# Weighed sums of a windowed attention as three products of split operands

## The reference

```python
q = (x @ Wq.T).reshape(B, T, H, Dh).transpose(0, 2, 1, 3)     # 16 heads of 128
k = (x @ Wk.T).reshape(B, T, Hkv, Dh).transpose(0, 2, 1, 3)   # 4 key heads
v = (x @ Wv.T).reshape(B, T, Hkv, Dh).transpose(0, 2, 1, 3)
q = _rms_norm(q, qn_w); k = _rms_norm(k, kn_w)                # then both are rotated
scores = jnp.einsum('bhgtd,bhkd->bhgtk', qg, k)
mask = (dist >= 0) & (dist <= WINDOW)                         # WINDOW = 64
att = jax.nn.softmax(jnp.where(mask, scores, min), axis=-1)
ctx = jnp.einsum('bhgtk,bhkd->bhgtd', att, v)
return out @ Wo.T                                             # out: ctx, heads side by side
```

## Time and profile before

| | |
|---|---|
| median of 3 runs | 1400.53 us (1397.14 to 1403.43) |
| the profiled execution | 1384.34 us |
| its span, first to last instruction | 1382.5 us |
| mean granted clock of PE | 0.949 |
| busy, share of the span | PE 88%, PEld 68%, DVE 69%, ACT 55%, POOL 44% |

### The profile page before, as it was taken

The page is one execution under the profiler, slowest core; times in us unless marked ns, Lnnn a source line. Parts: engine busy times, 40 slices in busy tenths (PEclk is TensorE's granted clock), DMA queues, the critical chain, the costliest instruction groups (busy, mean ns, idle before and its releaser), DMA issues. The chain is left out here.

```text
span 1382.5 us, 24786 instructions
## 1 busy us (share of the span) xinstructions
PE 1214.4 (88%) x7679; PEld 940.9 (68%) x7726; DVE 957.8 (69%) x1855; ACT 760.1 (55%) x1757; POOL 606.2 (44%) x745
## 2 busy tenths in 40 slices
PE   6895899989989985489998999989987999969998
PEld 5673444558888874367777777777774666648887
DVE  5999799856755458877777777777764767744443
ACT  5433477763555454566666666666662666633332
POOL 2000556552164454776666666676663343310000
PEclk9998899989999998699999999999997999989999
DMA  9001000010035314200000000000000000000000
GB/s 335 3 1 53 15 16 16 12 62 1 9 98 155 104 50 168 110 1 1 2 0 0 0 0 0 0 0 0 1 1 5 4 4 3 2 1 1 16 15 32
DMA packets 27422, 44.74 MB, mean 32 GB/s; under 512 B 5648, under 2 KB 22160, under 8 KB 25936
## 3 DMA queue, kind: packets, MB, share of 16 engines
q1 hardware_dynamic: 23888, 34.31, 7.2%
q0 software_dynamic: 3456, 9.44, 2.6%
HBM read 32.21 MB, written 9.44 MB: 30 GB/s over the span
## 5 line engine op out<-in xcount | busy, mean ns | idle before, releaser
L2334 ACT ACTIVATE wi_weights<-wi_psum,wi_bias,wi_scale 128x128 f32<-128x128 f32 x256 | 113.7, 454 | 120.2 <-DVE wi_bias L2454 120.2
L2109 POOL TENSOR_TENSOR wi_straight<-wi_straight,wi_crossed 128x512 f32<-128x512 f32 x80 | 103.0, 1288 | 10.9 <-DVE wi_crossed L2440 10.8
L978 DVE TENSOR_REDUCE gq_least<-gq_psum 128x4 f32<-128x512 f32 x128 | 84.6, 685 | 15.5 <-PE gq_psum L861 13.8
L2097 POOL TENSOR_TENSOR wi_scratch<-wi_sums,wi_eps 128x4 f32<-128x4 f32 x80 | 33.8, 422 | 129.8 <-DVE wi_sums L2413 128.4
L2098 POOL TENSOR_TENSOR wi_scale<-wi_scratch,minus_half 128x4 f32<-128x4 f32 x80 | 84.5, 1057 | 6.3
L2224 PE MATMUL wi_psum<-wi_k_t,wi_q_t 128*128 128x128 f32 x512 | 68.0, 276 | 20.8 <-ACT wi_q_t L2325 19.5
L940 ACT ACTIVATE gq_weights_t<-gq_psum 128x512 f32<-128x512 f32 x128 | 67.7, 601 | 23.4 <-PE gq_psum L881 23.1
L2175 PEld LDWEIGHTS wi_psum<-const,wi_straight 128*128 128x128 f32 x320 | 39.1, 142 | 54.6 <-issue 36.1
L2445 DVE TENSOR_REDUCE wi_top<-wi_psum 128x4 f32<-128x512 f32 x64 | 43.8, 684 | 45.8 <-PE wi_psum L2224 45.8
L2427 DVE TENSOR_TENSOR wi_straight<-wi_raw,rows 128x512 f32<-128x512 f32 x80 | 71.6, 895 | 0.0
L2119 POOL TENSOR_TENSOR wi_weights<-wi_weights,wi_inverse 128x512 f32<-128x512 f32 x64 | 66.4, 1038 | 9.5 <-remote 5.1
(11 more groups left out here) (410 smaller groups left out, 3780.3 us busy)
## 6 DMA issues: line engine op xcount, KB each, us to landing
slot_y<-ex_s_out SPq DMA_DIRECT2D x20, 256.0 KB, 2.2
x<-in_x_dram SPq DMA_DIRECT2D x4, 512.0 KB, 8.1
gate<-in_gate_dram SPq DMA_DIRECT2D x2, 1024.0 KB, 6.6
up<-in_up_dram SPq DMA_DIRECT2D x2, 1024.0 KB, 8.6
down<-in_down_dram SPq DMA_DIRECT2D x2, 1024.0 KB, 10.5
egu<-in_egu_dram SPq DMA_DIRECT2D x1, 2048.0 KB, 15.5
gq_keys_diagonal<-gq_key_parts SPq DMA_DIRECT2D x64, 32.0 KB, 1.9
wo<-in_wo_dram SPq DMA_DIRECT2D x1, 2048.0 KB, 8.8
```

The source lines that it names most:

```text
L978: dve.tensor_reduce(least[:, n // 2 % 2, n % 2, j, :], ps[:, j % 2, :].rearrange("p (v t) -> p v t", t=P), AX.X, ALU.min).then_inc(topped, 1)
L2109: added_up = pool.tensor_tensor(straight[:, at], straight[:, at], crossed[:, at], ALU.add)
L2334: act.activation(weights[:, g % 2, j, :], ps[:, SC + g % 2, j * P:j * P + P], ACT.Exp, bias=bias[:, g % 2, j:j + 1], scale=scale[:, g, j:j ...
```

## The change

Values and weights are split as well. ACT writes the values as `values_high`, and DVE takes `values_low` from PSUM (`split_values`), in step 1 behind `invert`, and for block 0 behind the casts. ACT rounds the turned weights into `weights_high` (`take_weights_high`, ahead of `weigh`), and DVE's copy at line 2461 becomes a subtraction into `weights_low`, which waits for ACT's rounding. `attend` makes three float32r products instead of one in float32. PE waits ahead of each q0 projection until the values of its block are split, since both use the same bank.

```diff
--- before.py
+++ after.py
@@ -1991,11 +1991,13 @@
 
         h_tok, h_high = sb("wi_h_tok", [P, 2, D]), sb("wi_h_high", [P, 2, KC, P], F32R)
         h_low = sb("wi_h_low", [P, 2, KC, P], F32R)
-        values = sb("wi_values", [P, 2, KVH * DH])
+        values_high = sb("wi_values_high", [P, 2, KVH * DH], F32R)
+        values_low = sb("wi_values_low", [P, 2, KVH * DH], F32R)
         raw, square = sb("wi_raw", [P, 3, 4, DH]), sb("wi_square", [P, 2, 4, DH])
         straight, crossed = sb("wi_straight", [P, 3, 4, DH]), sb("wi_crossed", [P, 3, 4, DH])
         q_t, k_t = sb("wi_q_t", [P, 2, 4, P]), sb("wi_k_t", [P, 2, KVH, P])
-        weights, weights_t = sb("wi_weights", [P, 2, 4, P]), sb("wi_weights_t", [P, 2, BANK])
+        weights = sb("wi_weights", [P, 2, 4, P])
+        weights_high, weights_low = sb("wi_weights_high", [P, 2, BANK], F32R), sb("wi_weights_low", [P, 2, BANK], F32R)
         out_high, out_low = sb("wi_out_high", [P, 2, 4, P], F32R), sb("wi_out_low", [P, 2, 4, P], F32R)
         raw_w = {"v": net.wv, "k": net.wk, "q": net.wq, "o": net.wo}
         w_high = {n: sb(f"wi_w{n}_high", w.shape, F32R) for n, w in raw_w.items()}
@@ -2028,6 +2030,8 @@
         turned_taken = sem("wi_turned_taken")
         turned_p = sem("wi_turned_p")
         turned_p_taken = sem("wi_turned_p_taken")
+        turned_p_high = sem("wi_turned_p_high")
+        values_split = sem("wi_values_split")
         scored = sem("wi_scored")
         bias_ready = sem("wi_bias")
         weighed = sem("wi_weighed")
@@ -2202,6 +2206,8 @@
                 if what == "v":
                     pe.wait_ge(turned_taken, number("h", t) + 1)
                     pe.wait_ge(h_low_ready, t + 1)
+                elif what == "q" and g == 0:
+                    pe.wait_ge(values_split, t + 1)
                 name = f"q{g}" if what == "q" else what
                 if isinstance(t, int) and t == 0:
                     split(name)
@@ -2230,8 +2236,11 @@
                 pe.wait_ge(turned_p_taken, U * t + g + 1)
                 need(pe, attended_taken, U * t + g)
                 need(pe, out_low_ready, U * t + g)
-                pe.matmul(ps[:, AV, :], values[:, s, g * DH:g * DH + DH], weights_t[:, g % 2],
-                          start=True, stop=True).then_inc(attended, 1)
+                of = slice(g * DH, g * DH + DH)
+                pe.matmul(ps[:, AV, :], values_high[:, s, of], weights_high[:, g % 2], start=True, stop=False)
+                pe.matmul(ps[:, AV, :], values_low[:, s, of], weights_high[:, g % 2], start=False, stop=False)
+                pe.matmul(ps[:, AV, :], values_high[:, s, of], weights_low[:, g % 2],
+                          start=False, stop=True).then_inc(attended, 1)
 
             def project_out(t, g):
                 pe.wait_ge(attended_taken, U * t + g + 1)
@@ -2294,7 +2303,7 @@
                 bank = ps[:, PJ + of_six(what, 0, g) % 2, :]
                 if what == "v":
                     need(act, attended, U * (t - 1))
-                    act.activation(values[:, s], bank, ACT.Copy).then_inc(proj_taken, 1)
+                    act.activation(values_high[:, s], bank, ACT.Copy).then_inc(proj_taken, 1)
                     return
                 n, at = of_five(what, t, g), slot(what, g)
 
@@ -2335,6 +2344,12 @@
                                    bias=bias[:, g % 2, j:j + 1], scale=scale[:, g, j:j + 1],
                                    accum_out=total[:, g % 2, j:j + 1]).then_inc(weighed, 1)
 
+            def take_weights_high(t, g):
+                w = U * t + g
+                act.wait_ge(turned_p, w + 1)
+                need(act, attended, w - 1)
+                act.activation(weights_high[:, g % 2], ps[:, bank_of("p", g), :], ACT.Copy).then_inc(turned_p_high, 1)
+
             def take_attended(t, g):
                 act.wait_ge(attended, U * t + g + 1)
                 need(act, output, U * t + g - 1)
@@ -2345,6 +2360,9 @@
                 for g in range(U):
                     for item in ahead(t, s, g, last):
                         take(*item)
+                    if g > 0 or not first:
+                        pt, _, pg = earlier(t, s, g, 1, U)
+                        take_weights_high(pt, pg)
                     weigh(t, g)
                     if g == 3 and not last:
                         take_turned("k", t + 1, 1 - s)
@@ -2369,6 +2387,7 @@
             take_turned("k", 0, 0)
             take_turned("q", 0, 0, 0)
             pairs(act, one)
+            take_weights_high(NB - 1, 3)
             take_attended(NB - 1, 3)
 
         @block.vector
@@ -2456,9 +2475,16 @@
 
             def take_weights(t, g):
                 w = U * t + g
-                dve.wait_ge(turned_p, w + 1)
+                dve.wait_ge(turned_p_high, w + 1)
                 need(dve, attended, w - 1)
-                dve.tensor_copy(weights_t[:, g % 2], ps[:, bank_of("p", g), :]).then_inc(turned_p_taken, 1)
+                dve.tensor_tensor(weights_low[:, g % 2], ps[:, bank_of("p", g), :],
+                                  weights_high[:, g % 2].bitcast(F32), ALU.subtract).then_inc(turned_p_taken, 1)
+
+            def split_values(t, s):
+                dve.wait_ge(proj_taken, of_six("v", t, 0) + 1)
+                need(dve, attended, U * (t - 1))
+                dve.tensor_tensor(values_low[:, s], ps[:, PJ + of_six("v", 0, 0) % 2, :],
+                                  values_high[:, s].bitcast(F32), ALU.subtract).then_inc(values_split, 1)
 
             def invert(t, g):
                 w = U * t + g
@@ -2490,6 +2516,8 @@
                         rotate(*item)
                         rotate_crossed(*item)
                     invert(t, g)
+                    if g == 1 and not last:
+                        split_values(t + 1, 1 - s)
                     if g == 1 and not first:
                         finish(t - 1)
                     if g > 0 or not first:
@@ -2512,6 +2540,7 @@
             dve.tensor_copy(ident_b[:], net.const[:, CONST["ident"]]).then_inc(tables_ready, 1)
             dve.tensor_copy(mask[:], net.const[:, CONST["window"]].unsqueeze(1)
                             .broadcast_to([P, 4, P])).then_inc(tables_ready, 1)
+            split_values(0, 0)
             for item in FIRST_ITEMS:
                 rotate(*item)
                 rotate_crossed(*item)
```

## The result

| | before | after |
|---|---|---|
| median, us (runs) | 1398.84 (1395.65 to 1403.43, 4) | 1410.69 (1409.36 to 1413.9, 4) |
| the profiled execution / its span | 1384.34 / 1382.5 | 1409.36 / 1407.6 |
| mean granted clock of PE | 0.949 | 0.952 |
| local attention, first to last product | 482.8 | 503.6 |
| experts' stage ahead of it | 248.1 | 257.5 |

The ratio is 1.0087, 95% interval 1.0056 to 1.0119: slower by under 1%, clear of no change. Stage lengths are taken from the start of the first to the start of the last of PE's products into the stage's PSUM tile.

What follows compares the result with a forecast made beforehand. A chain passing between PE, ACT and DVE was taken to bound the kernel. Fourteen blocks at 0.88 (12.3), start 1.7, block 0 1.3 and last block 1.7 gave +17.0 us: 1417.5 against the median 1400.53, range 1405 to 1428.

Steps and rivals of the forecast that it cites:

- rival 2: Half the cost is absorbed in DVE's short waits: 0.4 us a block, +8 with the ends, 1408 us; chance 0.22.
- The product: PE's weighed sum: three split products take 0.68 us instead of 0.86; only group 0's saving of 0.18 reaches the chain.
- The third weight load: PE's weighed sum: the extra load lies under the products and costs nothing; lying open, 0.10 to 0.20 us.
- Rounding in step 1: Group 0's weights: ACT's rounding makes DVE 0.68 us late and the weighed sum start 0.17 late; net +0.09 a block.
- rival 3: Weight loads lie open: three products take 1.28 us instead of 0.68, 9 us more, 1427 in all; chance 0.05.
- The values' rest: New DVE operation ahead of the q0 projection: PE stalls 0.22 us plus 0.10 for an open load, +0.32 a block.
- Rounding in step 2: Group 1's weights: DVE's subtraction starts 0.47 us late behind ACT's rounding, delaying DVE's stretch to bias(3); bounds 0.3 to 0.7.
- Steps 3 and 0: Rounding of groups 2 and 3: cost 0 a block, upper bounds 0.18 us (step 3) and 0.1 (step 0).
- Middle blocks: Sum of the block's terms: +0.88 us, 29.55 instead of 28.67; 12.3 over fourteen blocks.
- Start and block 0: Stage start +1.7 us, as values' rest queues behind DVE's casts; block 0's roundings and rest +1.3.
- Last block: No projections cover steps 2 and 3: three roundings of 0.47 to 0.64 us and 0.1 in the tail, +1.7.
- Rival 4: Shifted DVE operations meet POOL's, one meeting costing 1.0 us: 14 more, 1432 in all; chance 0.05.

Runs made afterwards that it cites:

- e3: Kernel before with three rounded products in the weighed sum, no rounding step of its own and no rests; ratio 0.9993, pair of blocks 57.22 us against 57.47.
- e5: Changed kernel with the values' rest taken behind step 1's bias instead of behind `invert`; ratio to the kernel before 1.0100, pair of blocks 58.80 us against 59.66.
- e4: Changed kernel with bias and the sums of k ahead of the weights' subtraction in step 2; ratio to the kernel before 1.0134, pair of blocks 59.61 us.
- e6: Changed kernel with bias alone ahead of the weights' subtraction in step 2; ratio to the kernel before 1.0156, pair of blocks 59.73 us.
- e10: e7 with bias and the sums of k ahead of the weights' subtraction in step 2; ratio to the kernel before 1.0021, pair of blocks 57.33 us.
- e2: Changed kernel run again without edits, against the kernel before; ratio 1.0147, stage 505.3 us.
- e11: e7 with bias, sums and q's straight product ahead of both rests in step 1; ratio to the kernel before 1.0062, pair of blocks 58.19 us.
- e7: e5 with only the third product waiting for the rest of the weights; ratio to the kernel before 1.0068, pair of blocks 58.22 us.

## Why the prediction was right, and where its terms were off

The direction and the mechanism held, and so did the range: +17.0 us was forecast against a profiled execution; the stage grew by 20.8. The median after, 1410.7, stands just under the forecast's own bounds (1411.5 to 1422.5) and lies in the range by what that allows for the spread of the runs and for rival 2. The forecast's growth, 1417.5 over 1400.53 or 1.0121, stands between the two measured ones, 1.0087 and 1.0147. That the first came out lower, though the stage grew by more than forecast, is chance and no merit of the sum. Step by step:

- **The product**: forecast 0.68 instead of 0.86, and 0.78 with the open load. Measured 0.70 (e3) and 0.80. Right, and that only one of four counts is right as well: e3 gains 0.13 a block.
- **The third weight load** at nothing: right. Each load after the first takes 0.19 under a product pace of 0.23 (758.44, 758.67), and rival 3's 1.28 for the weighed sum does not occur.
The Trainium skill, "TensorE: Matmul & The Clock Gate", section "The mechanism" (the prediction names the heading behind it), says that a load overlaps with products in flight only where it goes to another row group; the trace disagrees here too. The same section also lets a load run ahead into a background weight buffer, and no run here shows whether that is what happens.
- **Rounding in step 1**: forecast +0.17 at the weighed sum, measured +0.18. With the product, +0.12 instead of +0.09.
- **The values' rest**: this term was mis-sized: +0.32 forecast, +0.46 measured (0.36 and 0.10), 0.43 by e5. The rest started 0.05 later relative to the weighed sum than I had it (2.13 instead of 2.08), and from its end to the first product took 0.15 (760.92 to 761.07) where I had put the 0.04 of lag that ACT and DVE show behind PE. The open load, 0.10, was right. The upper bound given for the stall, 0.5 with DVE 0.2 later, is 0.42 by the prediction's own numbers; the measured 0.36 lies inside it.
- **Rounding in step 2**: forecast +0.47, measured +0.46 at the maximum of group 3, and DVE's wait is where it was forecast (0.45). But the reason given, "all of DVE's stretch to bias(3)", is incomplete: that stretch isn't without a stop, as DVE waits 0.31 for out_high in it (750.54 before) and its crossed product waits for POOL. e4 and e6 took the wait from DVE's stretch and gained nothing; e10, which moved the sums of k as well as bias and kept the weighed sum on time, gained all of it. The late subtraction delays bias, and with it ACT's exponentials, q_t and scores(3), and it delays the sums of k, and with them POOL; both chains end at the same operation. The size came out right because one late subtraction delayed both alike (by 0.47 at bias and at the sums).
- **Steps 3 and 0** at nothing: right (maximum(3) at 9.66 is explained by step 2 alone; the middle block's four terms of 0.12, 0.46, 0.46 and 0 leave 0.05 of the 1.09, of which 0.03 lies in the values projection).
- **Middle blocks**: 0.88 forecast, 1.09 measured; from the last q_t of block 0 to the k_t of block 15 it is 409.93 before and 424.81 after, 14.9 us instead of 12.3.
- **Start and block 0**: +3.0 forecast, +3.8 measured (42.47 to 46.25; 2.8 in e2). **Last block**: +1.7 forecast, +2.1 measured at full clock. 14.9, 3.8 and 2.1 make the 20.8.

The absolute 1417.5 stood at the profiled time plus the distance to the median. The median after was 1410.7 in the first comparison and 1416.7 in the second (five executions); the stage's growth of 1.5% agrees with the second. That the gap to the first comes from the spread of the other stages is argued from their lengths, not shown.

Rival 2 (half absorbed) would have made blocks of 29.07, against 29.83 by the pair: none of the three terms that make up a block's growth came out more than 0.01 smaller than forecast. Rival 4's 1.0 a block from POOL's meetings didn't come: straight lasts 1.67 at one place in the block, as before. It was near, though: in e6 the meeting moved, and POOL's joining grew.

## What to carry to other kernels

A cheaper product is worth only what it saves on the chain (here one in four), while each rounding and rest that it needs is a new hand-over, and most of those can lie on the chain (here three in a block). Let each product wait for its own operand, and take a rest that another engine stands still for as soon as its source is there: that gave back 0.7 us a block without removing an operation. Where moving an operation away from a wait gains nothing, look for a second chain that ends at the same instruction before calling the wait harmless; here two orders failed alone, and one of them paid once the other chain was free.

## What the runs showed of the hardware that was not expected

**The clock in the last block.** PE is busy for little more than half of the time there, and in some executions the granted clock falls to half before the stage's end (in e2 at 1069.1; in after at 1079.1, behind the stage's end). Windows of 10 us of e2, then of after:

```profile
1060.00:1070.00 10.00, 5.55 (x36) 4.39 (x35) 3.25 (x9) 5.79 (x20) 1.98 (x2) 0.96 0.00 0
1070.00:1080.00 10.00, 7.85 (x31) 6.77 (x31) 1.80 (x4) 1.19 (x2) 0.10 (x1) 0.50 0.00 0
```

```profile
1060.00:1070.00 10.00, 5.82 (x38) 4.53 (x37) 3.27 (x9) 5.80 (x20) 1.70 (x2) 1.00 0.00 0
1070.00:1080.00 10.00, 5.12 (x33) 4.15 (x33) 4.51 (x24) 1.19 (x2) 1.91 (x5) 0.96 0.02 7
```

The stage ends at 1079.1 in e2 and at 1076.4 in after. It is the same kernel at the same place, within 1 us, at 2.4 GHz in one execution and at 1.2 in the other, and the end takes 3.0 us more (32.54 and 35.50). The same explains most of what is odd in e11: its middle takes as long as e7's (414.68 and 414.87 from the last q_t of block 0 to the k_t of block 15), and its end, 35.14 at clock 0.83 instead of 32.20 at 1.00, and its start, 45.48 at 0.73 instead of 43.83 at 0.82, make up the 4.4 us. For the start this is argued: e10's takes 43.95 at 0.76, and e11's own order in block 0 may have a share.

**The experts' stage** took from 248.1 to 268.5 us in the profiled executions, with the same code: more than the whole effect studied. What sets it wasn't tried.

**POOL beside DVE.** In e6 POOL's joining took 1.74 us where it met DVE's straight product (748.62 and 748.19), against a median of 1.28 for its 80 cases; in e10 it took 1.77 in the same meeting.
The Trainium skill, "GPSIMD Engine Reference", section "1. Specifications", says that POOL's access to SBUF is shared with VectorE and contended by instructions with two SBUF inputs. Both operations have two, and the trace agrees.
